# The seam between an attention stage and its routed experts: order of the first gather, of the counts and of the first weights' split

## The reference, cut to what matters

```python
q, k, v = heads(xn @ wq.T), heads(xn @ wk.T), heads(xn @ wv.T)      # 16 heads of 16
q = (q @ fq1.T + b) * (q @ fq2.T + b); k = (k @ fk1.T + b) * (k @ fk2.T + b)
# causal linear attention in chunks of 64, a norm per head, then @ wo.T
probs = softmax(xn @ router_w.T)                                     # 8 experts
w = keep the largest probs of a token until their sum exceeds 0.9
out = sum over e of (silu(xn @ gate_w[e].T) * (xn @ up_w[e].T)) @ down_w[e].T * w[:, e]
return x + attention(xn) + out
```

## Time and profile before

| what | value |
|---|---|
| median of 3 runs | 766.76 us (766.34 to 768.1) |
| the profiled execution | 765.0 us, its span 763.3 us |
| mean granted TensorE clock | 0.973 of full speed |
| TensorE busy | 715.8 us, 94% of the span |
| VectorE, ScalarE, GpSimd busy | 495.6, 404.0, 346.1 us |
| chain that ended last, by engine | PE 79%, DVE 11%, issue 4%, DMA 2%, ACT 2% |

### The profile page before, as it was taken

How to read it: one execution, slowest core, us unless ns; L and a number is a source line. 1 busy time by engine, 2 the same in 40 slices (tenths; PEclk the granted TensorE clock), 3 DMA queues, 4 the chain that set the end, 5 groups by cost and what they waited for, 6 DMA issues and landing times.

```text
span 763.3 us, 19612 instructions
## 1 busy us (share of the span) xinstructions
PE 715.8 (94%) x6616; PEld 659.2 (86%) x6617; DVE 495.6 (65%) x1149; ACT 404.0 (53%) x923; POOL 346.1 (45%) x371
## 2 busy tenths in 40 slices
PE   8589999999999994799999999999999999999993
PEld 7467777777777773799999999999999999999992
DVE  5377887879788788365655754755754756656652
ACT  4236465555646546254655654655654655555551
POOL 3001202211120612266666766666766666666663
PEclk9799999999999998799999999999999999999997
DMA  2431211213120302543543643633643634543332
GB/s 93 131 85 48 66 56 55 59 52 111 34 77 28 76 9 70 178 101 58 110 97 58 136 70 56 145 63 57 134 72 57 144 63 79 120 63 57 63 60 31
DMA packets 51860, 59.58 MB, mean 78 GB/s; under 512 B 9344, under 2 KB 48256, under 8 KB 51840
## 3 DMA queue, kind: packets, MB, share of 16 engines
q0 software_dynamic: 19776, 27.16, 22.3%
q1 hardware_dynamic: 32064, 32.16, 14.2%
HBM read 37.15 MB, written 22.15 MB: 78 GB/s over the span
## 4 chain that ended last, share of the span: by engine, by line
PE 79%; DVE 11%; issue 4%; DMA 2%; ACT 2%; SPq 1%; POOL 0%; DVEq 0%; ACTq 0%; POOLq 0%
PE ring L1120 10%; PE ring L1121 10%; PE ring L1122 10%; PE A L1120 9%; PE A L1121 9%; PE A L1122 9%; DVE s_sb L801 4%; PE ring L1166 3%; PE S L1122 3%; PE S L1121 3%; PE S L1120 3%; PE A L1347 3%; PE ring L1188 3%; PE S L1194 2%; DMA xa<-x 1%
## 5 line engine op out<-in xcount | busy, mean ns | idle before, releaser
L473 POOL DMA_INDIRECT out<-ybuf,s_idx x98 | 161.8, 1651 | 62.6 <-POOL s_idx L469 46.6
L457 POOL DMA_INDIRECT xg<-gather_table,g_idx x100 | 100.5, 1005 | 88.2 <-issue 62.2
L1095 DVE TENSOR_TENSOR h_lo<-h,h_hi 128x256 fp32r<-128x256 f32 x196 | 83.5, 426 | 79.4 <-ACT h_hi L724 79.4
L724 ACT ACTIVATE h_hi<-h 128x256 fp32r<-128x256 f32 x196 | 82.0, 418 | 64.8 <-DVE h L1091 56.8
L1120 PE MATMUL ring<-w_hi,h_hi 128*128 128x256 f32 x392 | 113.7, 290 | 0.4 <-DVE h_lo L1095 0.4
L1120 PE MATMUL A<-gT_hi,w_hi 128*128 128x256 f32 x392 | 110.2, 281 | 1.8 <-DVE gT_lo L1064 1.8
L1121 PE MATMUL A<-gT_lo,w_hi 128*128 128x256 f32 x392 | 109.9, 280 | 0.0
L1122 PE MATMUL A<-gT_hi,w_lo 128*128 128x256 f32 x392 | 109.7, 280 | 0.0
L1122 PE MATMUL ring<-w_hi,h_lo 128*128 128x256 f32 x392 | 109.5, 279 | 0.0
L1121 PE MATMUL ring<-w_lo,h_hi 128*128 128x256 f32 x392 | 109.5, 279 | 0.0
L373 POOL TENSOR_TENSOR on_lo<-on,on_hi 128x512 fp32r<-128x512 f32 x15 | 19.3, 1288 | 143.4 <-ACT on_hi L534 143.4
(11 more groups left out here) (221 smaller groups left out, 2055.1 us busy)
## 6 DMA issues: line engine op xcount, KB each, us to landing
w_raw<-wffn SPq DMA_DIRECT2D x72, 192.0 KB
xa<-x SPq DMA_DIRECT2D x8, 512.0 KB, 4.7
gather_table<-xna SPq DMA_DIRECT2D x8, 512.0 KB, 3.1
xr<-x SPq DMA_DIRECT2D x8, 512.0 KB, 4.2
out<-yout SPq DMA_DIRECT2D x8, 512.0 KB
out<-ybuf,s_idx POOLq DMA_INDIRECT x104, 3.9
xg<-gather_table,g_idx POOLq DMA_INDIRECT x100
w_raw<-wqk_nat SPq DMA_DIRECT2D x1, 512.0 KB, 4.9
```

The costliest lines, as they stand in the source:

```text
L457: pool.indirect_dma_start(out=xg[:, sub, :], out_offset=None, in_=table, in_offset=bass.IndirectOffsetOnAxis(ap=g_idx[:, sub:sub + 1], axi ...
L473: pool.indirect_dma_start(out=out, out_offset=bass.IndirectOffsetOnAxis(ap=s_idx[:, sub:sub + 1], axis=0), in_=ybuf[:, sub, :], in_offset= ...
L724: a.activation(h_hi[:, ic, :], h[:, ic, :], ACT.Copy).then_inc(hhi_ok, 1)
L1095: v.tensor_tensor(h_lo[:, ic, :], h[:, ic, :], h_hi[:, ic, :].bitcast(F32), ALU.subtract).then_inc(hlo_ok, 1)
```

## The change

In the first round ScalarE makes the eight high pieces of expert 0 in two groups of four (behind `keys_by_token` and behind the first `squares`), and VectorE the eight low pieces (behind `softmax_head` and behind `slots`). They are gone from the seam. In the last round VectorE's masks 6 and 7 stand ahead of the one-hot rows, and TensorE's last index table behind the values and the first mean squares. VectorE makes the index table first, then a memset that frees the gather, then the counts, which a new semaphore `count_ok` releases. GpSimd gathers for the first tile right behind its index copy, ahead of its `outputs_low` of the last block; it reads the counts after that, and its loop over experts has the first expert written out. All four engines that read the counts wait for `count_ok`. ScalarE's closing order is changed.

```diff
 # GpSimd
+            g.memset(idx_all[:, NE * (NT // P):], 0)
             g.memset(yout[:, 0, 0:1], 0.0).then_inc(yout_free, DMA)
...
             add_zeros(2)
-            outputs_low(NBLK - 1, 0)
...
-            link(g.memset(idx_all[:, NE * (NT // P):], 0))
             pool.wait_ge(tab_ok, 1)
...
             next_index(pool.snap(done))
+            gather()
+            outputs_low(NBLK - 1, 0)
+            pool.wait_ge(count_ok, 1)
             tiles = TileCounts(pool, n_tiles)
...
-            with pool.Fori(0, NE) as e:
+            n = tiles.now()
+            turn(0, 0, True, True)
+            with pool.Fori(1, n) as j:
+                turn(0, j)
+            next_index(NT // P)
+            tiles.step()
+            with pool.Fori(1, NE) as e:
 # ScalarE, round_of
                 keys_by_token(s, 0)
+                if first:
+                    first_high_pieces(0)
                 queries2(s, 1)
...
                 squares(s, 0)
+                if first:
+                    first_high_pieces(1)
 # ScalarE, closing
-            act.wait_ge(w_in, PIECES * DMA)
-            for piece in range(PIECES // 2):
-                high_piece(0, piece * PW)
+            head_rstd(NBLK - 1, 0)
             squares(NBLK - 1, 1)
-            for piece in range(PIECES // 2, PIECES):
-                high_piece(0, piece * PW)
-            head_rstd(NBLK - 1, 0)
+            heads_hi(NBLK - 1, 0)
             head_rstd(NBLK - 1, 1)
-            heads_hi(NBLK - 1, 0)
             heads_hi(NBLK - 1, 1)
 # VectorE, round_of
                 softmax_head(s, chain)
+                if first:
+                    for piece in range(PIECES // 2):
+                        first_low_piece(piece)
                 state(s, 0)
...
                     slots(s, 1, chain)
-                    one_hot(s, 0)
-                    one_hot(s, 1)
                     masked_scores(s, 6)
                     state(s, 1)
                     masked_scores(s, 7)
+                    one_hot(s, 0)
+                    one_hot(s, 1)
                     return
...
                 slots(s, 1, chain)
+                if first:
+                    for piece in range(PIECES // 2, PIECES):
+                        first_low_piece(piece)
                 head_norm(s, 0, chain)
 # VectorE, closing: the index table, the memsets, then the counts
+            add_indices(NBLK - 1, last_idx_bank)
...
+            v.memset(h[:, :, 3:4], 0.0).then_inc(wt_ok, 1)
+            v.memset(h[:, :, 0:1], 0.0).then_inc(h_free, IC)
             chain.link(v.tensor_scalar(cum[0:1, 0, :], base[0:1, 0, :], float(FT - 1), None, ALU.add))
...
+            v.tensor_scalar(n_tiles[:, 0:NE], cnt_i[:, :], MIN_TILES, None, ALU.max).then_inc(count_ok, 1)
             head_norm(NBLK - 1, 0, chain)
 # TensorE
-                if last:
-                    pe.wait_ge(y_ok, 2 * s + 1)
-                    slot_tokens(s, last_idx_bank)
                 values(s, 2)
                 values(s, 3)
...
                 mean_squares(s, 0)
                 if last:
+                    pe.wait_ge(y_ok, 2 * s + 1)
+                    slot_tokens(s, last_idx_bank)
                     mean_squares(s, 1)
                     return
...
+            pe.nop().then_inc(xg_free, 1)
             round_of(NBLK - 1, False, True)
...
-            pe.nop().then_inc(xg_free, 1)
...
+            pe.wait_ge(count_ok, 1)
             tiles = TileCounts(pe, n_tiles)
```

More of the change, by code:

```diff
@@ L247, in build @@
                  "ls_ok ex_ok sel_ok rank_ps rank_ok slot_ok lo_ok oh_ok idx_ps idx_ok w_ok table_in wtab_in "
-                 "dve_step pool_step tab_ok w_in wsplit "
+                 "dve_step pool_step tab_ok count_ok w_in wsplit "
                  "gathered xg_free ghi_ok glo_ok gu_ps silu_ok h_free hhi_ok hlo_ok y_ps ya_ok yd_ok "
@@ L255, in build @@
          ls_ok, ex_ok, sel_ok, rank_ps, rank_ok, slot_ok, lo_ok, oh_ok, idx_ps, idx_ok, w_ok, table_in, wtab_in,
-         dve_step, pool_step, tab_ok, w_in, wsplit,
+         dve_step, pool_step, tab_ok, count_ok, w_in, wsplit,
          gathered, xg_free, ghi_ok, glo_ok, gu_ps, silu_ok, h_free, hhi_ok, hlo_ok, y_ps, ya_ok, yd_ok,
@@ L477, in _, with turn @@
             next_index(pool.snap(done))
+            gather()
+            outputs_low(NBLK - 1, 0)
+            pool.wait_ge(count_ok, 1)
             tiles = TileCounts(pool, n_tiles)
-            def turn(e, j, first=False):
+            def turn(e, j, first=False, gathering=False):
                 col = pool.snap(e * (NT // P) + j * SUB)
-                gather()
+                if not gathering:
+                    gather()
                 with pool.If(pool.snap(done) > LAG - 1):
@@ L605, in outputs_copy, with first_high_pieces @@
                              ACT.Copy).then_inc(y_ok, 1)
+            def first_high_pieces(part):
+                act.wait_ge(w_in, PIECES * DMA)
+                for piece in range(part * PIECES // 2, (part + 1) * PIECES // 2):
+                    high_piece(0, piece * PW)
             def round_of(s, first, last):
@@ L730, in _ @@
             tokens_hi(0)
+            act.wait_ge(count_ok, 1)
             tiles = TileCounts(act, n_tiles)
@@ L1027, in _ @@
             round_of(NBLK - 1, False, True, chain)
[L1028 to L1032, removed]
             add_indices(NBLK - 1, last_idx_bank)
@@ L1039, in _ @@
             v.tensor_copy(idx_all[:, 0:NE * (NT // P)], idx_f[:, :, :].rearrange("p e n -> p (e n)")).then_inc(tab_ok, 1)
-            for piece in range(PIECES // 2):
-                first_low_piece(piece)
             dve.wait_ge(table_in, DMA * NBLK)
             dve.wait_ge(wtab_in, DMA * NBLK)
+            v.memset(h[:, :, 3:4], 0.0).then_inc(wt_ok, 1)
             v.memset(h[:, :, 0:1], 0.0).then_inc(h_free, IC)
-            v.memset(h[:, :, 3:4], 0.0).then_inc(wt_ok, 1)
-            for piece in range(PIECES // 2, PIECES):
-                first_low_piece(piece)
+            chain.link(v.tensor_scalar(cum[0:1, 0, :], base[0:1, 0, :], float(FT - 1), None, ALU.add))
+            chain.link(v.tensor_copy(cnt_i[:, :], cum[0:1, 0, :]))
+            chain.link(v.tensor_scalar(cnt_i[:, :], cnt_i[:, :], FT.bit_length() - 1, None, ALU.arith_shift_right))
+            chain.link(v.memset(n_tiles[:, NE:NE + 1], MIN_TILES))
+            v.tensor_scalar(n_tiles[:, 0:NE], cnt_i[:, :], MIN_TILES, None, ALU.max).then_inc(count_ok, 1)
             head_norm(NBLK - 1, 0, chain)
@@ L1101, in _ @@
             tokens_lo(0)
+            dve.wait_ge(count_ok, 1)
             tiles = TileCounts(dve, n_tiles)
```

## The result

The changed kernel took **769.96 us** (median of 9 runs, 768.79 to 773.79). The kernel before took 767.34 us in the 9 runs beside them. The ratio is **1.0039 [1.0023, 1.0055]**: 2.6 us slower, where 0.6 was forecast, and past the 0.2% that a measurement of this kernel can tell. The profiled execution took 769.96 us, its span 768.2 (765.0 and 763.3 before). I read the changed trace in the order of the prediction.

A forecast was written before the change was run, and what follows sets the result against it. TensorE's work was taken as the bound, so only round 0 and the closing stretch could matter: +1.2 - 0.6 = +0.6 us, giving 767.4 us for the median (766.76 before), range 764.8 to 769.5.

The forecast's parts named there:

- the last of part 3: Expert stage: GpSimd's first expert written out costs nothing, since GpSimd has 12 us of TensorE work per tile as cover.
- the stage fixed: Expert stage: the last 438 us are a fixed length of TensorE work, with one wait of 0.3 us.
- Part 1: Round 0: expert 0's split moved there; low pieces 4 to 7 ahead of the head norm delay round 1 by 1.2 us.
- Part 2: Closing round: the new order starts the last output projection 0.6 us earlier, between 1.5 earlier and no gain.
- 0.25 us off: Closing round: deducted from the 0.85 us gain because GpSimd's and VectorE's on_lo both end near 303.7.
- Part 3: First tile: early gather starts expert matmuls 2.9 us earlier, but expert 1's weights land late and hide it; no gain.
- estimate of 5.6 us: Expert 1's weight loads: the skill's figures give 5.6 us for 1.57 MB; the trace's 8.2 us was used instead.
- the clock falls in the first tile: Rival, first tile: TensorE's waits drop the clock, so the second tile starts slow; 2.1 us more, 769.5 us; chance 0.20.
- round 0 absorbs the split: Rival, round 0: the moved split costs nothing, only the closing gain is left, 766.2 us; chance 0.13.
- the weights don't gate: Rival, first tile: weights land earlier, so the gather's 2.9 us come through, 765.1 us; chance 0.17.

## Why the prediction was wrong

**The step that failed is the last of part 3**: "GpSimd's unrolled first expert: no cost … GpSimd has 12 us of TensorE work per tile to cover its own". No row gives these 12 us: the tile has 8.83 us and GpSimd's turn 8.63, so GpSimd is the second bound of the expert stage, and that it held its lead in the kernel before was luck of the order. I had looked at TensorE's waits there, found none, and called the stage fixed. The earlier trace rows said that no wait was there, not how near one was; the row that says it is GpSimd's own wait for w_tok. The code is not the cost, the order in the seam is: 1.4 to 2.3 us in the two profiles, and 2.4 us between the medians when GpSimd's part is taken back.

**Part 1, +1.2 us:** right in place and cause, and about right in size: 0.9 us between profiles in which the clock fell in this stretch, 0.4 between those in which it did not, 1.6 between the medians with and without it. The high pieces and the low pieces 0 to 3 cost nothing that shows.

**Part 2, -0.6 us:** wrong sign, +0.5 at the output projection, between profiles whose clock rose early. I had both on_lo end near 303.7, with 0.25 us off; they began together (304.55 and 304.56) and VectorE's took 1.82 us, 1.1 more than alone. The clock at 1.2 GHz through the output projection made that +1.0 at the last residual, and landing weights, which scatter by 0.9 us between two profiles of the kernel before, +1.2 to +2.1 at the second tile. How much of this reaches the time is not shown, since taking the collision away alone changed the time by 0.15 us, give or take 1. The prediction also had no term for when the clock rises behind the state matmuls, which moves the output projection by over 1 us between profiles of one closing order (18.16 and 19.24 in the old one).

**Part 3, no gain from the first gather:** right. Expert matmuls 1.4 us earlier (3 forecast, since the output projection is later), 4.3 us of wait for h_lo (3 to 5 forecast), 7.6 us of ScalarE's wait for weights, and 6.3 us won when the weights come early. From their first issue to the split 8.96 us passed (313.17 to 322.13); the prediction's estimate of 5.6 us doesn't agree here either. The section of the Trainium skill that it draws on (DMA: Bandwidth & Descriptors, Anatomy of one DMA) gives its figures for one transfer issued by GpSimd; these are eight, issued by SyncE one after another, so the estimate stretched them too far.

**The rivals:** that the clock falls in the first tile came true in part; the earlier trace rows had shown it, and 19 matmuls took 4.00 us at 1.2 GHz, but by the second tile it was at 2.4 GHz again. That round 0 absorbs the split, or that the weights don't gate, did not happen.

The terms from the profiles (0.9, then 1.2 to 2.1, then 1.4 to 2.3) add up to more than the 2.6 us of the medians. The two profiles of the kernel before lie 2.3 and 1.4 us under the medians of the runs beside them, so differences of profiles are too large here, and I give the split no finer than that. **Open:** what first makes GpSimd late. With its order of before all six profiles have the short tail; with the changed one two of eleven have it too (early weights, 426.74, and ScalarE's old order with on_lo first, 426.90), while on_lo first alone does not (428.36). Most of these kernels have one profile, and that of the early weights is of its fastest run, so that an exception may be one of the execution and not of the kernel.

## What to carry to other kernels

An engine that shows no wait on the bounding engine can still be a hair from it: compare its turn with the bound's, and read how long *it* waits, since that is the lead a reordering can spend. The gather started earlier was worth nothing here while another input of the same step, the weights, came as late as before; find the last input first. Moving the weights' eight load issues ahead of the last round was worth 5.2 us. Before two profiles are compared stretch by stretch, see that the granted clock was the same in that stretch. When two engines are given halves of one job, look at whether both would read the same memory at the same time, and let one start early.

## What the runs showed of the hardware that I had not expected

Two like subtractions on VectorE and GpSimd don't slow each other a little: the second stood still for the whole of the first (1.82 us against 0.69). Beside the same kind of subtraction on VectorE, GpSimd's issue of an indirect gather took 1.33 against 0.97 us, and a copy of 128x2 indices 0.48 against 0.20. Of SyncE's eight weight loads in a row in the changed kernel, the second took 0.94 us to issue, the others 0.43 to 0.51; in the two profiles of the kernel before the second took 0.54 and 0.87.
